# Matrix-memory layer: gate steps of a group spread over two slots, one activation table, floor and norm product on GpSimd, residual at the slot's end

## The reference

```python
x = jnp.concatenate([q, k, v], axis=-1)
ig = (x @ Wi + bi).transpose(0, 2, 1)[..., None]
fg = (x @ Wf + bf).transpose(0, 2, 1)[..., None]
...
log_f = jax.nn.log_sigmoid(fg)
log_f_cum = jnp.concatenate([jnp.zeros((b, nh, 1, 1), q.dtype), jnp.cumsum(log_f, axis=2)], axis=2)
fg_mat = log_f_cum - jnp.transpose(log_f_cum, (0, 1, 3, 2))
log_fg = jnp.where(ltr, fg_mat[:, :, 1:, 1:], -jnp.inf)
log_D = log_fg + jnp.transpose(ig, (0, 1, 3, 2))
max_log_D = jnp.max(log_D, axis=-1, keepdims=True)
D = jnp.exp(log_D - max_log_D)
qk = jnp.einsum('bhsd,bhtd->bhst', qh, kh) / jnp.sqrt(jnp.asarray(dh, q.dtype))
C = qk * D
normalizer = jnp.maximum(jnp.abs(C.sum(-1, keepdims=True)), jnp.exp(-max_log_D))
h = jnp.einsum('bhst,bhtd->bhsd', C / (normalizer + EPS), vh)
mu = h.mean(-1, keepdims=True)
var = ((h - mu) ** 2).mean(-1, keepdims=True)
hn = (h - mu) * jax.lax.rsqrt(var + EPS) * ln_scale.reshape(1, nh, 1, dh)
```

## Time and profile before

| What | us |
|---|---|
| median of 3 runs | 5205.83 |
| lowest and highest of them | 5203.84, 5206.42 |
| profiled execution, its own time | 5204.22 |
| span of its trace | 5202.6 |
| PE busy over the span | 4947.2 (95%) |
| DVE busy | 4244.9 (82%) |
| ACT busy | 3750.0 (72%) |
| POOL busy | 2154.7 (41%) |

### The profile page before, as it was taken

How to read it: one execution, slowest core, us unless ns; L and a number is a source line. 1 busy time by engine, 2 the same in 40 slices (tenths; PEclk the granted TensorE clock), 3 DMA queues, 4 the chain that set the end, 5 groups by cost and what they waited for, 6 DMA issues and landing times. The chain is left out here.

```text
span 5202.6 us, 113763 instructions
## 1 busy us (share of the span) xinstructions
PE 4947.2 (95%) x38146; PEld 3686.3 (71%) x38146; DVE 4244.9 (82%) x10272; ACT 3750.0 (72%) x9646; POOL 2154.7 (41%) x2774
## 2 busy tenths in 40 slices
PE   7999999999999999999999997879999989989999
PEld 4777777777777777777777776868756767778666
DVE  4999999999999999999999995779722368878523
ACT  4999999999999999999999984648713434456233
POOL 2555555555555555555555552431133300011342
PEclk9999999999999999999999998979999999999999
DMA  5500000000000000000000001010022372010234
GB/s 178 160 3 7 6 2 7 6 2 7 7 4 6 6 7 3 7 6 3 7 6 2 7 1 37 16 34 2 2 87 81 125 234 92 2 43 19 80 103 164
DMA packets 178112, 204.53 MB, mean 39 GB/s; under 512 B 28539, under 2 KB 165628, under 8 KB 176896
## 3 DMA queue, kind: packets, MB, share of 16 engines
q1 hardware_dynamic: 161840, 159.47, 9.9%
q0 software_dynamic: 12960, 34.63, 1.9%
q10 hardware_dynamic: 2736, 3.09, 0.2%
HBM read 158.33 MB, written 114.16 MB: 52 GB/s over the span
## 5 line engine op out<-in xcount | busy, mean ns | idle before, releaser
L1856 POOL TENSOR_TENSOR gsa_qka<-gsa_qka,gsa_tmpa 128x256 f32<-128x256 f32 x64 | 47.8, 746 | 316.1 <-DVE gsa_tmpa L1419 316.1
L1890 POOL TENSOR_TENSOR gsa_qkb<-gsa_qkb,gsa_tmpb 128x256 f32<-128x256 f32 x64 | 47.7, 746 | 307.0 <-DVE gsa_tmpb L1557 307.0
L1156 PE MATMUL PSA<-gsa_wo,gsa_sgb 128*128 128x256 f32 x512 | 129.3, 396 | 24.5 <-DVE gsa_r0b L1463 24.5
L1300 PE MATMUL PSA<-gsa_wo,gsa_sga 128*128 128x256 f32 x512 | 128.2, 393 | 25.0 <-DVE gsa_r0a L1596 25.0
L465 ACT ACTIVATE ffn0b_sl<-PSA 128x512 f32<-128x512 f32 x40 | 23.9, 597 | 172.9 <-PE PSA L165 172.8
L2389 POOL TENSOR_TENSOR mlstm_rs<-mlstm_wide,mlstm_neghalf 128x16 f32<-128x16 f32 x32 | 93.4, 2919 | 132.4 <-DVE mlstm_wide L2257 132.4
L270 DVE TENSOR_TENSOR ffn0b_hidden<-ffn0b_sl,PSA 128x512 f32<-128x512 f32 x40 | 27.5, 686 | 130.6 <-ACT ffn0b_sl L465 130.6
L1109 PE MATMUL PSA<-XT,gsa_wa 128*128 128x512 f32 x256 | 123.4, 605 | 7.8 <-DMA gsa_wa<-in_w_heads 7.4
L410 DVE COPY ffn0b_hT<-PSA 128x256 f32<-128x256 f32 x71 | 30.1, 425 | 123.2 <-PE PSA L206 123.2
L410 DVE COPY ffn1b_hT<-PSA 128x256 f32<-128x256 f32 x71 | 30.1, 425 | 121.5 <-PE PSA L206 121.5
L1156 PEld LDWEIGHTS PSA<-gsa_wo,gsa_sgb 128*128 128x128 f32 x512 | 93.1, 192 | 49.6 <-DVE gsa_r0b L1463 39.3
(11 more groups left out here) (803 smaller groups left out, 19203.0 us busy)
## 6 DMA issues: line engine op xcount, KB each, us to landing
pairs<-in_blank SPq DMA_DIRECT2D x2, 35904.0 KB, 125.7
ffn0b_XS<-pairs SPq DMA_DIRECT2D x71, 132.0 KB, 2.1
ffn1b_XS<-pairs SPq DMA_DIRECT2D x71, 132.0 KB, 2.1
gsa_wa<-in_w_heads SPq DMA_DIRECT2D x64, 128.0 KB, 2.0
X<-in_x SPq DMA_DIRECT2D x8, 512.0 KB, 7.9
mlstm_CX<-in_ctx SPq DMA_DIRECT2D x32, 128.0 KB, 2.1
ffn0b_WGU<-results SPq DMA_DIRECT2D x8, 512.0 KB, 4.8
ffn0b_WD<-results SPq DMA_DIRECT2D x8, 512.0 KB, 6.7
```

The lines of the kernel that those rows point to most:

```text
L1156: last = nc.tensor.matmul(PS[5 + j // 2][:, (j % 2) * 256:(j % 2) * 256 + 256], tile(SGb[:, :], j), WO[:, :], start=True, stop=True)
L1300: last = nc.tensor.matmul(PS[1 + j // 2][:, (j % 2) * 256:(j % 2) * 256 + 256], tile(SGa[:, :], j), WO[:, :], start=True, stop=True)
```

## The change

- `gates` on DVE is split. `forget` (LF and the sum F) comes one slot earlier, with s - 8; `maxima` (U and M) stays at s - 9. FM moves to POOL as `floor`.
- `turn_floor` on PE and `floors` on ACT come one slot later (s - 8 for s - 7, s - 7 for s - 6), and the waits on their counts are shifted to match.
- `finish` on DVE is split in three. `scale` (T1 = H * rs) comes right behind `mask`, ahead of `normalize` and `widths`. The product with LNB moves to POOL as `weigh`. `residual` stays at the slot's end, behind `product`.
- POOL's list is now `row_power` (s), `floor` once a group, `weigh` (s - 13), `head_power` (s - 12).
- One table that has both the exponential and the logarithm is loaded at the start of ACT's list.

```diff
@@ PE: gates(n) @@
-                    floors = min((n + 1 - LEAD) // 4 + 1, GROUPS)
+                    floors = min((n - LEAD) // 4 + 1, GROUPS)
@@ PE: turn_floor(g) @@
-                    pe.wait_ge(floor_by_dve, g + 1)
-                    pe.wait_ge(gated_by_act, min(4 * g - 1 + LEAD, TILES))
+                    pe.wait_ge(floor_by_pool, g + 1)
+                    pe.wait_ge(gated_by_act, min(4 * g + LEAD, TILES))
@@ PE: slots @@
-                    if (s - 7) % 4 == 0 and 0 <= s - 7 < TILES:
-                        turn_floor((s - 7) // 4)
+                    if (s - 8) % 4 == 0 and 0 <= s - 8 < TILES:
+                        turn_floor((s - 8) // 4)
@@ DVE @@
-                def gates(g):
+                def forget(g):
                     b = g % 2
                     dve.wait_ge(logf_by_act, 3 * g + 3)
                     nc.vector.scalar_tensor_tensor(LF[b][:, :], FB[b][:, :], 0.0, LN1[b][:, :], ALU.min, ALU.subtract).then_inc(logf_by_dve, 1)
                     dve.wait_ge(logf_by_dve, g + 1)
+                    if g >= 2:
+                        dve.wait_ge(floor_by_pool, g - 1)
                     nc.vector.tensor_tensor_scan(F[b][:, :], RST[:, 0:512], LF[b][:, :], 0.0, ALU.mult, ALU.add).then_inc(cumf_by_dve, 1)
+
+                def maxima(g):
+                    b = g % 2
                     dve.wait_ge(cumf_by_dve, g + 1)
...
                     nc.vector.tensor_tensor_scan(M[b][:, :], RST[:, 512:1024], U[b][:, :], -1e30, ALU.add, ALU.max).then_inc(cummax_by_dve, 1)
-                    dve.wait_ge(cummax_by_dve, g + 1)
-                    if g >= 2:
-                        dve.wait_ge(floor_by_pe, g - 1)
-                    nc.vector.tensor_tensor(FM[b][:, :], F[b][:, :], M[b][:, :], ALU.add).then_inc(floor_by_dve, 1)
...
-                def finish(n):
+                def scale(n):
                     b = n % 2
                     dve.wait_ge(rs_by_pool, n + 1)
                     nc.vector.tensor_tensor(T1[b][:, :, :], H[b][:, :, 0:16], rs[b][:, :].unsqueeze(2).to_broadcast([128, 16, 16]), ALU.mult).then_inc(scaled_by_dve, 1)
-                    dve.wait_ge(scaled_by_dve, n + 1)
-                    nc.vector.tensor_tensor(T1[b][:, :, :], T1[b][:, :, :], by_head(LNB[:, :]), ALU.mult).then_inc(weighed_by_dve, 1)
-                    dve.wait_ge(weighed_by_dve, n + 1)
+
+                def residual(n):
+                    b = n % 2
+                    dve.wait_ge(weighed_by_pool, n + 1)
                     nc.vector.tensor_tensor(rows(n), rows(n), T1[b][:, :, :].rearrange("p h d -> p (h d)"), ALU.add).then_inc(residual_by_dve, 1)
...
+                    if (s - 8) % 4 == 0 and 0 <= s - 8 < TILES:
+                        forget((s - 8) // 4)
                     if (s - 9) % 4 == 0 and 0 <= s - 9 < TILES:
-                        gates((s - 9) // 4)
+                        maxima((s - 9) // 4)
                     if 0 <= s - 10 < TILES:
                         mask(s - 10)
+                    if 0 <= s - 13 < TILES:
+                        scale(s - 13)
...
                     if 0 <= s - 13 < TILES:
-                        finish(s - 13)
+                        residual(s - 13)
@@ ACT @@
+                nc.scalar.preload_act_table_set("natural_log_exp_and_others")
...
-                    if (s - 6) % 4 == 0 and 0 <= s - 6 < TILES:
-                        floors((s - 6) // 4)
+                    if (s - 7) % 4 == 0 and 0 <= s - 7 < TILES:
+                        floors((s - 7) // 4)
@@ POOL @@
+                def floor(g):
+                    b = g % 2
+                    pool.wait_ge(cummax_by_dve, g + 1)
+                    if g >= 2:
+                        pool.wait_ge(floor_by_pe, g - 1)
+                    nc.gpsimd.tensor_tensor(FM[b][:, :], F[b][:, :], M[b][:, :], ALU.add).then_inc(floor_by_pool, 1)
+
+                def weigh(n):
+                    b = n % 2
+                    pool.wait_ge(scaled_by_dve, n + 1)
+                    nc.gpsimd.tensor_tensor(T1[b][:, :, :], T1[b][:, :, :], by_head(LNB[:, :]), ALU.mult).then_inc(weighed_by_pool, 1)
+
-                for s in range(TILES + 12):
+                for s in range(TILES + 13):
                     if 0 <= s < TILES:
                         row_power(s)
+                    if (s - 9) % 4 == 0 and 0 <= s - 9 < TILES:
+                        floor((s - 9) // 4)
+                    if 0 <= s - 13 < TILES:
+                        if s == 13:
+                            pool.wait_ge(loads, 144)
+                        weigh(s - 13)
                     if 0 <= s - 12 < TILES:
                         head_power(s - 12)
```

More of the change, by code:

```diff
@@ L2070, in mlstm @@
         cummax_by_dve = signal("cummax_by_dve")
-        floor_by_dve = signal("floor_by_dve")
+        floor_by_pool = signal("floor_by_pool")
         floor_by_pe = signal("floor_by_pe")
@@ L2088, in mlstm @@
         scaled_by_dve = signal("scaled_by_dve")
-        weighed_by_dve = signal("weighed_by_dve")
+        weighed_by_pool = signal("weighed_by_pool")
         residual_by_dve = signal("residual_by_dve")
```

## The result

The changed kernel takes 5188.22 us (median of 8 executions, 5182.72 to 5191.54); the kernel before took 5205.94 us beside it (8 executions, 5203.84 to 5207.00). The ratio is 0.9968 with a 95% interval of 0.9958 to 0.9978: 17.7 us or 0.34% less. The forecast was 5187 us.

A forecast was written before the change was run, and what follows sets the result against it. PE had most of the work (6.65 us a tile) but wasn't alone; DVE's gate work made it wait. Terms -1.5 - 4.0 - 15.5 - 3.0 + 2.5 + 4.7 = -16.8 us took 5204.2 to 5187.4 us, said as 5187; range 5169 to 5201 us.

The forecast's parts named there:

- The hold: GpSimd's `weigh` delays the first short instruction of `widths` on DVE: between 0 and 0.74 us, taken as 0.55 us.
- queue rival: GpSimd's queue: `weigh` ahead of the power delays `scale` once over 2.8 us; 5223 us at 4.0 us, chance 0.03.
- power rival: The power on GpSimd also holds DVE's residual, making the layer 28 us longer: 5215 us, chance 0.02.
- I take it to stay: PE's clock stays at its higher level behind longest gaps of 1.1 us; a group takes 30.1 us.
- three signs: Wrong if plain slots are 6.65 us, clock is lower behind short gaps, or the preload puts off the first tiles.
- clock rival: PE's clock falls in two gaps of 1.1 us, 1.2 us twice a group: 5201 us, chance 0.2.
- three places of a group: Where a group loses 6.6 us on PE: wait before `turn_floor`, lower clock behind it, wait in the `log_forget` slot.
- no hold: GpSimd's product delays no `widths` instruction, so plain slots are PE's 6.65 us: 5175 us, chance 0.2.
- the tail: Last four slots, 3413.45 to 3440.47: loop longer by 0.33 + 0.55 us, taken as 2.5 us more (of 3.5).
- place (c): Slot with `log_forget`: PE waits 0.64 us, with ACT's table loads starting the product 1.27 us late.
- the start's 1.5 us: Up to the first mask: one load and FM less, against the preload; 1.5 us less, between 0 and 2.8.
- up to 0.7: Early `forget` on DVE could have waited up to 0.7 us for ACT's logarithm with the load in place.

The follow-up runs named there:

- e1: Changed kernel with the product with LNB back on DVE, behind the main product: ratio 0.9951 to the kernel before, layer 273.3 us.
- e2: Changed kernel with `scale` moved behind `widths`, product with LNB still on GpSimd: ratio 0.9944 to the kernel before, layer 270.1 us.
- e7: Kernel before with the preload of the common table as its only change: ratio 0.9974 to the kernel before, layer 285.2 us.
- e4: Changed kernel without the preload of the common table: ratio 0.9972 to the kernel before, layer 289.1 us.
- e3: Changed kernel with `finish` as in the kernel before, all on DVE behind the main product: ratio 0.9947 to the kernel before, layer 268.3 us.
- e8: Changed kernel with unread matmuls filling PE's gaps in slots with gate work and the last six slots: 5206.30 us, ratio 1.0004 to the kernel before.

## Why the prediction was right, step by step

**What held.** The sum of the layer (-16.8 against -16.5 us), and every stretch but the last four slots within 1 us. The hold of GpSimd's product on the widths' first step: taken as 0.55 us of a possible 0.74, measured 0.53 us, and e1 removes it by removing that product. Mask to product start 3.60 us (3.06 + 0.55). DVE's two slots with gate work 7.77 and 7.80 us (7.8). PE no longer waits before `turn_floor`; GpSimd's product takes 0.84 us beside normalize and 0.73 us in the last slots, which have none. There the hold falls on the widths' second step instead, at the same size (L2247 at 3396.57 takes 0.72 us). The queue rival and the power rival are dead: the residual at 3228.23 takes 0.41 us beside the heads' power (3227.26 to 3230.18), as the earlier trace rows let expect.

The Trainium skill ("SBUF — State Buffer", section "Who interferes with whom") has the port pair taken by VectorE instructions with two SBUF inputs and by some with one (`tensor_scalar`), but not by one whose other input is PSUM. The runs agree for the first and the last: the widths' step was held, the main product in e2 wasn't. In e2 a normalize (`tensor_scalar`) beside the floor took 0.70 us in place of 0.40 (timelines of POOL and DVE):

```profile
3237.83 1.27 POOL L2403 TENSOR_TENSOR mlstm_FM<-mlstm_F,mlstm_M 128x512 f32<-128x512 f32 x1
3238.55 0.70 DVE L2209 TENSOR_SCALAR mlstm_xn<-X,mlstm_mv,mlstm_rstd 128x256 f32<-128x256 f32 x1
```

So it was held as well. The page ties this to the instruction's two-port modes. Whether the normalize runs in one, no row shows; alone it takes 0.41 us, as long as a two-input product of its size (L2263). The residual beside the power, at 0.41 us, doesn't fit the rule.

**What failed: "I take it to stay".** The clock didn't stay at its higher level behind gaps of 1.1 us; this is one of the three signs by which I said that I would be wrong. I had only the rows with 0.64 and 1.68 us, and took the nearer end for the middle. Three traces of the changed kernel show the same: groups 11 to 15 and 15 to 19 take 31.3 and 30.9 us, the two before them 29.9 and 30.0. So it costs about 1 us in two of five groups, not 2.4 us in each, as my clock rival had it; a fall at the first of the two gaps only slows an engine that would wait anyway. That the sum came out is in part luck, since a second error cancelled this one: the fifth group (19 to 23) has no statistics in its last two slots and takes 28.2 us, where I gave it 30.1 like the others. Without the luck the stretch would have been off by 2 us. My last step was a slip too: 16.8 us under the 5205.8 us of the median is 5189 us, and 5187 us is what belongs to the profiled execution. The three places of a group in the kernel before add up to 7.0 us, not to 6.6 us, which no later term used.

**Mis-sized: "no hold" and the tail.** I priced an absent hold at 12 us, 8 of them in masks 3 to 23. e1, which frees it but leaves 0.4 us more on DVE, gives 8.1 us in the layer, 3.8 of them there; e2, without that 0.4 us, gives 11.3 us and 4.9, where the clock takes its part. In the last four slots I took 2.5 us of a possible 3.5; it was 4.2. The loop bounds three of them, at 7.6 to 7.7 us; PE itself bounds the fourth (8.21 us, all at the lower level, with `turn_floor` now in it). Slot by slot they are 0.9, 0.5, 1.9 and 0.9 us longer than before. The 1.9 us are the hold and `scale` (0.9) and the clock: that slot had stood at the higher level before and took 5.67 us.

**The table load: wrong in size and cause.** I named 0.64 us a group, PE's visible wait at place (c), and a share of the start's 1.5 us. In e7 the load alone gave 12.7 us of the layer: 8.0 in the slots before the gate masks, since the late product also pushed the gate work behind it, 2.8 at the start, and 1.9 elsewhere. What I did have right is the new order: `forget` had little to wait for with the loads in place (0.24 us in e4, "up to 0.7"). My sum for the group held only because I built the new group from durations, without subtracting this term.

**Not asked.** The prediction costed the split of `finish` as a part of the whole, and saw its price (loop 0.88 us longer, tail and drain 7 us), but never compared with leaving it out. My own terms would have given that: the earlier trace rows show a loop of 6.02 us under PE's 6.65: 0.63 us of slack, against 0.33 + 0.55 us put in.

## What to carry to other kernels

When a change has several parts, price it also without each part. Here one bundle of three held -20.9, -8.8 and +13.1 us in the layer, in the order in which they were taken out, and its own sum of -16.5 hid that nearly half of the gain was given back. A step that is moved off a busy engine is only free if it doesn't land inside the loop that bounds the plain slots: move it to where the engine waits anyway (behind the loop's last step), and look at which of the neighbour's instructions it will run beside. Even so placed it needn't pay (e2 against e3). A late step's price isn't the wait that it shows on the busiest engine, but what is queued behind it on its own.

## What the runs showed of the hardware

- A table load (1.28 us) on ACT lay on the path for 1.35 to 1.41 us in five of seven groups of the kernel before (e7), though ACT was busy for only 61% of masks 3 to 23 (100.83 of 165.96 us in the earlier trace rows). With the gate work in two slots the same loads cost 0.24 us in four groups (e4).
- A 128x16 instruction of DVE with both inputs in SBUF waited for a whole GpSimd product of 128x256 to end (0.71 for 0.17 us), and ended 0.03 us behind it. A 128x1024 product with PSUM on one side wasn't touched (1.22 us in e2), nor was the residual beside the heads' power (0.41 us).
- GpSimd was held too: the row power of one column takes 0.54 us in most slots, and 1.56 us beside the scan with both inputs in SBUF (3230.13 above; 1.55 or 1.56 us in four of 32).
- The clock fell behind PE gaps of 0.82, 1.03 and 1.27 us, and stayed behind 1.02 us (3266.17 in the changed kernel) and 0.87 us (once in e2). In e8 it fell once with no gap ahead. The gap alone doesn't decide it.
- A 128x128 by 128 columns f32 matmul is two instructions and 0.24 to 0.26 us at the higher level (e8: 3.84 us for 16, 1.83 us for 7).
